# Row maxima turned on their own, and probabilities cast two heads at a time, in the first cross attention of a decoder

## The reference

```python
q = rope(x @ Wq, pos); k = rope((ctx @ Wkv)[..., :512], pos); v = (ctx @ Wkv)[..., 512:]
s = einsum("bqhd,bkhd->bhqk", q, k) / sqrt(16)
o = softmax(s, axis=-1) @ v                      # 32 heads
x = layernorm(x + o @ Wout + bout)
```

## Time and profile before

| | us |
|---|---|
| median of 3 runs (lowest, highest) | 3235.99 (3232.26, 3239.41) |
| the profiled execution | 3238.21 |
| its span, first to last instruction | 3236.4 |
| `xattn0`, from the first exponential to the end of its heads | 776 to 1220 |
| `attn1`, the same with its start | 1880 to 2170 |

### The profile page before, as it was taken

The page is one execution under the profiler, slowest core; times in us unless marked ns, Lnnn a source line. Parts: engine busy times, 40 slices in busy tenths (PEclk is TensorE's granted clock), DMA queues, the critical chain, the costliest instruction groups (busy, mean ns, idle before and its releaser), DMA issues. The chain is left out here.

```text
span 3236.4 us, 64362 instructions
## 1 busy us (share of the span) xinstructions
PE 2811.6 (87%) x24738; PEld 1992.0 (62%) x24738; DVE 2087.0 (64%) x4863; ACT 1765.5 (55%) x3780; POOL 1430.2 (44%) x1539
## 2 busy tenths in 40 slices
PE   5999999967888887999999888989999999965786
PEld 3666666644666665777777666657666666642343
DVE  6677777667777766555555457766555555555896
ACT  4555555546888884333332267755444444454785
POOL 3444444435888884444444425552111112213563
PEclk8999999989999997999999989999999999988998
DMA  5000000000000013000000011002001110022000
GB/s 171 27 1 2 1 1 1 1 19 25 2 2 2 2 47 97 24 8 8 1 1 1 1 57 41 15 2 76 27 27 33 34 40 1 1 80 70 14 20 27
DMA packets 47124, 81.75 MB, mean 25 GB/s; under 512 B 5730, under 2 KB 15972, under 8 KB 46692
## 3 DMA queue, kind: packets, MB, share of 16 engines
q1 hardware_dynamic: 46820, 77.64, 7.3%
HBM read 73.44 MB, written 4.19 MB: 24 GB/s over the span
## 5 line engine op out<-in xcount | busy, mean ns | idle before, releaser
L1146 POOL TENSOR_TENSOR c_pT<-c_prob,c_pT 128x512 f16<-128x512 f32 x256 | 293.3, 1159 | 66.4 <-ACT c_pT L1096 65.7
L2029 POOL TENSOR_TENSOR c_prob<-c_prob,c_inv 128x512 f32<-128x512 f32 x128 | 133.1, 1043 | 301.4 <-DVE c_inv L2247 301.4
L789 DVE SCALAR_TENSOR_TENSOR a_pT<-psT,a_kvh_t,a_pT 128x256 f16<-128x256 f32 (+1 forms) x256 | 94.6, 411 | 168.9 <-ACT a_pT L695 168.9
L1339 ACT ACTIVATE c_prob<-psT 128x512 f32<-128x512 f32 x256 | 156.2, 610 | 73.1 <-PE psT L1268 52.1
L1146 POOL TENSOR_TENSOR a_pT<-a_prob,a_pT 128x384 f16<-128x384 f32 x128 | 120.8, 949 | 156.8 <-ACT a_pT L1096 156.1
L1423 DVE TENSOR_REDUCE c_peak<-psS 128x2 f32<-128x512 f32 x256 | 167.1, 683 | 11.5 <-PE psS L1249 9.3
L1096 ACT CAST c_pT<-c_prob 128x512 f16<-128x512 f32 x256 | 159.9, 625 | 0.0
L2163 ACT ACTIVATE c_prob<-c_prob,c_negmax 128x256 f32<-128x256 f32 x256 | 127.8, 501 | 55.9 <-DVE c_negmax L2239 54.9
L488 POOL TENSOR_TENSOR a_q_rot<-a_q_cos,a_q_sin 128x512 f32<-128x512 f32 x64 | 86.7, 1355 | 160.7 <-DVE a_q_sin L808 160.7
L507 POOL TENSOR_TENSOR a_prob<-a_prob,a_inv 128x128 f32<-128x128 f32 x128 | 52.4, 409 | 221.8 <-DVE a_inv L782 221.8
L1679 POOL TENSOR_TENSOR f_ch<-f_h,f_c 128x256 f32<-128x256 f32 x88 | 76.2, 866 | 141.9 <-DVE f_h L1896 141.7
(11 more groups left out here) (625 smaller groups left out, 11319.9 us busy)
## 6 DMA issues: line engine op xcount, KB each, us to landing
c_feed<-in_L_ffn_w1T SPq DMA_DIRECT2D x16, 512.0 KB, 3.7
c_feed<-in_L_ffn_w2T SPq DMA_DIRECT2D x16, 512.0 KB, 3.7
x_all<-in_x SPq DMA_DIRECT2D x8, 512.0 KB, 7.1
a_ring<-in_L_attn_WqT SPq DMA_DIRECT2D x8, 512.0 KB, 5.3
a_ring<-in_L_attn_WoutT SPq DMA_DIRECT2D x8, 512.0 KB, 3.8
a_feed<-in_L_xattn_Wq SPq DMA_DIRECT2D x8, 512.0 KB, 3.6
c_feed<-in_L_xattn_Wo SPq DMA_DIRECT2D x8, 512.0 KB, 4.2
c_feed<-in_L_ffn_w3T SPq DMA_DIRECT2D x8, 512.0 KB, 3.6
```

Source lines behind the costliest of these rows:

```text
L789: last = dve.scalar_tensor_tensor(pT[1][:, r, m, m * P:N], T[:, m * N + m * P:(m + 1) * N], kvh_t[:, b % 2, m, H + h:H + h + 1], pT[0][:, ...
L1146: pool.tensor_tensor(pT[1][:, c % NPH, :], prob[:, c % NPX, :], pT[0][:, c % NPH, :], ALU.subtract)\
L1339: act.activation(prob[:, c % NPX, :], ST[c % 2][:, 0:EW], ACT.Exp).then_inc(s.e_done, 1)
L2029: pool.tensor_tensor(prob[:, h % NPB, :, :], prob[:, h % NPB, :, :], inv[:, h % NPB, :].rearrange("p (n a) -> p n a", a=1).broadcast_to([P ...
```

## The change

In the layers that are not causal (`by_row`, so `xattn0` alone) the maxima no longer go through `q_stack`. DVE writes them into a tile `peak` of 128 columns per half, eight of which are a group's heads and the rest zero. PE turns this tile (two f32 turns of 128 x 128 for a group), DVE copies the 256 columns to `peak_rows` times -1/1024, and the scores with keys on the partitions get a second product: `pick`, a 128 x 128 tile that is 1024 in the row of the head and zero elsewhere, with `peak_rows`. The copy over `qS` on ACT, the product of `fill_slots` and the clearing of the slot on POOL go. `q_stack` has one buffer instead of two.

ACT casts the probabilities of two heads with one instruction, at even slots (`TOGETHER = 2`), and `prob` has four buffers instead of three. `pv` runs six slots after its head's scores instead of seven.

In `attn1`, `fill_slots` takes the later maximum with one reduction into `late` and writes the slots with two products instead of one.

```diff
-    NPX, NPH = 3, 6
+    NPX, NPH = 3 if causal else 4, 6
+    by_row = not causal
+    NQS = 1 if by_row else 2
+    TOGETHER = 2 if by_row else 1
...
-        q_stack = sc.sb("q_stack", [P, 2, NT, H, 4, D], F16)
+        q_stack = sc.sb("q_stack", [P, NQS, NT, H, 4, D], F16)
-        peak = sc.sb("peak", [P, H, PIECES], F32)
+        peak = sc.sb("peak", [P, 2, NT, P] if by_row else [P, H, PIECES], F32)
+        peak_rows = sc.sb("peak_rows", [P, 2, N], F16) if by_row else None
+        pick = sc.sb("pick", [P, GH, P], F16) if by_row else None
...
         def round_p(eng, copy, c):
-            eng.wait_ge(s.e_done, c + 1)
-            if c >= NPH:
-                eng.wait_ge(s.pv_done, c - NPH + 1)
-            copy(pT[0][:, c % NPH, :], prob[:, c % NPX, :]).then_inc(p_high(c)[0], 1)
+            last = c + TOGETHER - 1
+            eng.wait_ge(s.e_done, last + 1)
+            if last >= NPH:
+                eng.wait_ge(s.pv_done, last - NPH + 1)
+            copy(pT[0][:, c % NPH:c % NPH + TOGETHER, :], prob[:, c % NPX:c % NPX + TOGETHER, :]).then_inc(s.p_hi_act, 1)
...
-                    if kind == "q":
-                        pool.memset(q_stack[:, b % 2, n, :, 3, 0:1], 0.0).then_inc(s.slot_clear, 1)
...
+                def turn_peak_rows(b, g):
+                    pe.wait_ge(s.m_done, b * H + (g + 1) * GH)
+                    for n in range(NT):
+                        last = pe.transpose(bank_of("peak", b, g)[:, n * P:(n + 1) * P], peak[:, g % 2, n, :],
+                                            G.ident[:, :])
+                    last.then_inc(s.bank_ready, 1)
...
-                                         start=True, stop=not causal, skip_group_check=True)
-                        if causal:
+                                         start=True, stop=False, skip_group_check=True)
+                        if by_row:
+                            last = pe.matmul(out, pick[:, h % GH, :], peak_rows[:, h // GH % 2, q0:N], start=False, stop=True,
+                                             skip_group_check=True)
+                        else:
...
                 def q_stack_is_free(b):
-                    if b >= 2:
-                        act.wait_ge(s.bank_ready, use["peak", b - 2, NG - 1] + 1)
+                    if b >= NQS:
+                        act.wait_ge(s.bank_ready, (last_sk(b - 1, "q") if by_row else use["peak", b - 2, NG - 1]) + 1)
...
-                    if 0 <= t - 1 < B * H:
-                        round_p(act, act.copy, t - 1)
+                    if 0 <= t - TOGETHER < B * H and t % TOGETHER == 0:
+                        round_p(act, act.copy, t - TOGETHER)
...
                 def fill_slots(b, g):
                     heads = slice(g * GH, (g + 1) * GH)
                     dve.wait_ge(s.m_done, b * H + (g + 1) * GH)
-                    if causal:
-                        step(dve.tensor_tensor(peak[:, heads, 1], peak[:, heads, 1], peak[:, heads, 2], ALU.max))
-                    dve.tensor_tensor(q_stack[:, b % 2, :, heads, 3, 0], peak[:, heads, 0:NT].rearrange("p h n -> p n h"),
-                                      shift[:, 0:1].rearrange("p (n h) -> p n h", n=1).broadcast_to([P, NT, GH]),
-                                      ALU.mult).then_inc(s.slot_done, 1)
+                    step(dve.tensor_reduce(late[:, :], peak[:, heads, 1:3], X_AXIS, ALU.max))
+                    slots = q_stack[:, b % NQS, :, heads, 3, 0]
+                    scale = shift[:, 0:1].broadcast_to([P, GH])
+                    dve.tensor_tensor(slots[:, 0, :], peak[:, heads, 0], scale, ALU.mult)
+                    dve.tensor_tensor(slots[:, 1, :], late[:, :], scale, ALU.mult).then_inc(s.slot_done, 1)
+
+                def move_peaks(b, g):
+                    dve.wait_ge(s.bank_ready, use["peak", b, g] + 1)
+                    if NG * b + g >= 2:
+                        dve.wait_ge(s.st_ready, (NG * b + g - 1) * GH)
+                    dve.tensor_scalar(peak_rows[:, g % 2, :], bank_of("peak", b, g)[:, 0:N], -1.0 / SHIFT, None, ALU.mult)\
+                        .then_inc(s.bank_dve, 1)
...
-                     "peak": 28, "PV": 7}, G.c0, G.c0.end)
+                     "peak": 28, "PV": 6}, G.c0, G.c0.end)
```

More of the change, by code:

```diff
@@ L994, in small_attention @@
         prob = sc.sb("prob", [P, NPX, EW], F32)
-        peak = sc.sb("peak", [P, H, PIECES], F32)
-        shift = sc.sb("shift", [P, 1], F32)
+        peak = sc.sb("peak", [P, 2, NT, P] if by_row else [P, H, PIECES], F32)
+        late = sc.sb("late", [P, GH], F32) if causal else None
+        shift = None if by_row else sc.sb("shift", [P, 1], F32)
+        peak_rows = sc.sb("peak_rows", [P, 2, N], F16) if by_row else None
+        pick = sc.sb("pick", [P, GH, P], F16) if by_row else None
         inv = sc.sb("inv", [P, NT, GH], F32)
@@ L1060, in frees_bank @@
                 return "act" if sk_uses[n][0] == "q" else "dve"
-            return "act" if kind == "peak" else "dve"
+            return "act" if kind == "peak" and not by_row else "dve"
         use, freed, hi_at, v_at = {}, [], {}, {}
@@ L1120, in _ @@
             def _(pool):
-                pool.memset(shift[:, :], -1.0 / SHIFT).then_inc(s.zeroed, 1)
                 pool.memset(q_stack[:, :, :, :, 3, :], 0.0).then_inc(s.zeroed, 1)
-                pool.memset(k_stack[:, :, :, 3, 1:D], 0.0).then_inc(s.zeroed, 1)
-                pool.memset(k_stack[:, :, :, 3, 0:1], SHIFT).then_inc(s.zeroed, 1)
+                if by_row:
+                    pool.memset(k_stack[:, :, :, 3, :], 0.0).then_inc(s.zeroed, 1)
+                    pool.memset(peak[:, :, :, :], 0.0).then_inc(s.zeroed, 1)
+                else:
+                    pool.memset(shift[:, :], -1.0 / SHIFT).then_inc(s.zeroed, 1)
+                    pool.memset(k_stack[:, :, :, 3, 1:D], 0.0).then_inc(s.zeroed, 1)
+                    pool.memset(k_stack[:, :, :, 3, 0:1], SHIFT).then_inc(s.zeroed, 1)
                 pool.memset(v_ones[0][:, :, :, :, D:VW], 1.0).then_inc(s.zeroed, 1)
@@ L1136, in stack_lo @@
                     pool.wait_ge(s.rot_hi, u + 1)
-                    out, hi = (q_stack[:, b % 2, n, :, 1, :], q_stack[:, b % 2, n, :, 0, :]) if kind == "q" else \
+                    out, hi = (q_stack[:, b % NQS, n, :, 1, :], q_stack[:, b % NQS, n, :, 0, :]) if kind == "q" else \
                         (k_stack[:, n, :, 2, :], k_stack[:, n, :, 0, :])
-                    if kind == "q":
-                        pool.memset(q_stack[:, b % 2, n, :, 3, 0:1], 0.0).then_inc(s.slot_clear, 1)
                     pool.tensor_tensor(out, part[:, u % 2, 0, :].rearrange("p (h d) -> p h d", d=D), hi, ALU.subtract)\
@@ L1311, in _ @@
                         elif kind == "peak":
-                            turn_peaks(b, n)
+                            (turn_peak_rows if by_row else turn_peaks)(b, n)
                         elif kind == "o":
@@ L1350, in stack_hi @@
                     heads = H if kind == "q" else KVH
-                    out = q_stack[:, b % 2, n, :, 0:3:2, :] if kind == "q" else k_stack[:, n, :, 0:2, :]
+                    out = q_stack[:, b % NQS, n, :, 0:3:2, :] if kind == "q" else k_stack[:, n, :, 0:2, :]
                     view = src.rearrange("p (h d) -> p h d", d=D)
@@ L1366, in _ @@
                         turned_stack = kind == "sk" and frees_bank(kind, n) == "act"
-                        if kind in ("x", "o", "v", "kv", "peak") or turned_stack or (kind == "q" and not from_ctx):
+                        turned_peaks = kind == "peak" and not by_row
+                        if kind in ("x", "o", "v", "kv") or turned_stack or turned_peaks or (kind == "q" and not from_ctx):
                             bank = bank_of(kind, b, n)
@@ L1391, in _ @@
                             move_stack(act.copy, b, n).then_inc(s.bank_act, 1)
-                        elif kind == "peak":
+                        elif turned_peaks:
                             act.copy(qS[:, b % 2, GB * n:GB * (n + 1), :],
@@ L1422, in rowmax @@
                     S = SB[a % 2][:, 0:EW].rearrange("p (r m) -> p r m", r=PIECES)
-                    dve.tensor_reduce(peak[:, h, :], S, X_AXIS, ALU.max).then_inc(s.m_done, 1)
+                    group = a // GH
+                    if by_row and group >= 2 and h % GH == 0:
+                        dve.wait_ge(s.bank_ready, use[("peak", *divmod(group - 2, NG))] + 1)
+                    top = peak[:, group % 2, :, h % GH] if by_row else peak[:, h, :]
+                    dve.tensor_reduce(top, S, X_AXIS, ALU.max).then_inc(s.m_done, 1)
                 def fill_slots(b, g):
@@ L1467, in low @@
                     elif kind == "q":
-                        st = q_stack[:, b % 2, n, :, :, :]
+                        st = q_stack[:, b % NQS, n, :, :, :]
                         dve.memset(st[:, :, 3, 0:1], 0.0)
@@ L1531, in _ @@
                             move_stack(dve.tensor_copy, b, n).then_inc(s.bank_dve, 1)
+                        elif kind == "peak" and by_row:
```

(3 more changed lines are left out.)

15 lines of the change are left out of this document (9 added, 6 removed).

## The result

The changed kernel takes 3253.99 us in the median of 5 runs (3246.51 to 3258.48), the kernel before 3235.99 (3232.26 to 3240.19). The ratio is 1.0054, 95% interval [1.0043, 1.0065]: slower by 18 us. The forecast was 3263, its range 3222 to 3286.

What follows compares the result with a forecast made beforehand. No engine was taken as full: the bound moves within each period, through waits among POOL, ACT, PE and DVE. 3.6 us a period summed to +27 on 3236.0, so 3263 us in the median, range 3222 to 3286.

Steps and rivals of the forecast that it cites:

- the ring: First cross attention: low part, exponential, pair cast, low part again takes 2.87 us per pair against 2.44, POOL idling 0.60.
- First cut: Part of each sequence's period from head 0's exponential to head 10's: POOL's idle gaps add +1.3 us, ends 0 and +2.
- Fourth cut: Slots 27 to next head 0: late cast behind Q's projection leaves POOL without work, +1.5 us, between 0 and 2.6.
- Product and peaks: Second cut (head 10 to slot 21): extra matmuls less earlier bank, +0.5 us; third (slots 21 to 27): DVE's copy, +0.3.
- Sum: 3.6 us per period, 25 for seven sequences, +1.3 for the last, 1 for attn1: +27 us in all.
- the DVE stall: Removed DVE product, 229 to 4573 ns, contends with GpSimd; its replacement never stalls, giving back at most about 4 us.
- attn1: The other layer: one tiny DVE instruction more per group, 32 in all, 0 to 7 us of work, taken as 1.
- Start: The 1024-column DVE write and changed memsets before the first stack is turned: between -1 and +1 us, taken as 0.
- Rival (a): ACT is what bounds and its relief wins, half of 38 us counting: 3217 us, chance 0.24.
- Rival (b): Ring as described, but lumps of PE cover it and copies given back pay for PE's steps: about 3236 us, chance 0.12.
- Rival (c): PE becomes the bound outright, 55 us more less at most 14 of turns: 3277 us, chance 0.06.
- Rival (d): The DVE product's stall mattered more than its waits show, 17 us given back in full: 3246 us, no own chance.

Runs made afterwards that it cites:

- e2: Kernel before the change plus the pair cast, four prob buffers and the product with V six slots behind, maxima the old way: 3256.2 us, ratio 1.0067.
- e3: Changed kernel with both heads cast as soon as the second exponential is issued, one slot sooner: 3229.7 us, ratio 0.9984 to the kernel before.
- e6: Changed kernel with six prob buffers instead of four, pair cast left in its place: 3237.1 us, ratio 1.0009 to the kernel before.
- e7: Changed kernel with one cast per head, keeping its four prob buffers: 3221.1 us, ratio 0.9959 to the kernel before.
- e4: Changed kernel without the matmul that adds the maxima to the turned scores, so maxima are not subtracted: 3250.9 us, ratio 1.0051 to the kernel before.
- e8: Kernel before the change with four prob buffers instead of three and nothing else: 3216.1 us, ratio 0.9940.
- e9: Kernel before the change with four prob buffers in the first cross attention and attn1's new fill: 3212.9 us, ratio 0.9940.
- e5: Changed kernel with attn1's old fill, one product of maxima by scale instead of two small ones: 3260.7 us, ratio 1.0076 to the kernel before.
- e1: Changed kernel with single casts, three prob buffers and the product with V seven slots behind, so the new maxima alone: 3233.4 us, ratio 0.9991 to before.
- e10: e9 with the maxima scaled by a constant in the instruction in both layers, one SBUF operand instead of two: 3213.6 us, ratio 0.9937 to before.
- e11: e9 plus the pair cast at odd slots and the product with V six slots behind: 3226.0 us, ratio 0.9971 to before.

## Why the prediction was right, and where its sizes were off

The direction and the main mechanism, the ring, held; some of the smaller terms came out right for other reasons. By its own steps:

- **The ring.** Forecast 2.87 us per pair with 0.60 idle on POOL and a cast of 1.00 to 1.06; found 2.86, 0.58 and 1.04. That this ring is the cause is shown four ways: put alone into before it costs 22 us (e2), and a sooner place (e3), more buffers (e6) or single casts (e7) each take away 17 to 33 us.
- **First cut** +1.3, found +1.2. The gap behind the high stack was put at 1.4; it is 1.47 at 952.33.
- **Fourth cut** +1.5, found +1.5, by an idle time of POOL of 1.46 at 939.43. Together these two are 2.8 in the forecast and 2.8 in e2 (17.2 and 12.2 against 15.9 and 10.7). The fourth is the same without the product (e4) and with six buffers (e6), so the late cast makes it, as forecast.
- **Product and peaks** +0.5 and +0.3, found +0.5 and +0.25 in after's cuts. The numbers are better than the reasons. In the second cut the product costs 1.3 (21.08 against 19.77 in e4) where 1.1 was forecast, the pair cast adds 0.3 (20.86 in e2), which the forecast left out, and the relief is about 1.1 where 0.6 was forecast. In the third cut the forecast blamed DVE's new copy. But e4, which keeps that copy and lacks the product, takes 10.18, less than before's 10.37, so the product makes the increase, and the +0.3 came out by luck. PE's step is 0.96 (957.74 to 958.70 in after) as forecast. The peaks' copy takes 411 to 426 ns with no outlier.
- **Sum.** 3.6 a period was forecast and 3.45 found in plain periods. The whole came to 18 us and not 27. In the stage the seven periods differ by +1.6, -0.8, +3.5, +3.8, +1.8, +3.4, +3.2 and the last sequence by +2.2, together +18.6 (rounded terms) where 26 was forecast. Of the 8 that are missing, 5.9 are in the next point. About 2 are in the first period, which was taken as a full one: by cuts it differs by -0.05, -0.56, -0.05 and +2.2, so the first cut did not grow at all; why is open. The last sequence grew by 0.9 more than forecast.
- **The term that was mis-sized: what before itself loses.** The forecast took every period of before as plain and counted nothing for what the change could give back. The periods with -0.8 and +1.8 are those in which before is long, 61.75 and 59.20 us where a plain one takes 57.53: 4.2 and 1.7, or 5.9 us. They have two causes. The first is the DVE stall, which the forecast bounded at 4 us and counted as nothing: the first cut of the long period takes 18.47 instead of 15.93, 2.5 more, and that includes a stretch at half the clock right behind the stall (836.38 to 839.79). In before's timeline of DVE and of POOL:

```profile
831.50 4.57 DVE L1430 TENSOR_TENSOR c_q_stack<-c_peak,c_shift 128x16 f16<-128x16 f32 x1
835.94 0.68 DVE L1423 TENSOR_REDUCE c_peak<-psS 128x2 f32<-128x512 f32 x1
```

```profile
829.10 1.26 POOL L1132 TENSOR_TENSOR c_part<-c_part 128x512 f32<-128x512 f32 x1
830.33 2.26 POOL L1146 TENSOR_TENSOR c_pT<-c_prob,c_pT 128x512 f16<-128x512 f32 x2
832.54 0.23 POOL L1140 MEMSET c_q_stack<- 128x32 f16 x1
832.62 1.14 POOL L1141 TENSOR_TENSOR c_q_stack<-c_part,c_q_stack 128x512 f16<-128x512 f32 x1
833.73 2.25 POOL L1146 TENSOR_TENSOR c_pT<-c_prob,c_pT 128x512 f16<-128x512 f32 x2
```

  It ends at 836.07, and POOL's unbroken work at 835.98. The second cause is TensorE's clock, of which the forecast had no term. In both long periods the granted clock is 0.50 for 3.41 us in the fourth cut, where PE does the projection of Q without a pause, and that cut takes 12.36 instead of 10.68 us, 1.7 more each time. The rows are the two stretches and the fourth cut of the first of these periods:

```profile
877.34:880.75 3.41, 3.41 (x10) 1.21 (x9) 1.41 (x2) 1.84 (x3) 3.41 (x4) 0.50 0.00 0
1051.42:1054.83 3.41, 3.41 (x14) 1.22 (x11) 1.59 (x2) 2.02 (x3) 3.41 (x4) 0.50 0.00 0
876.37:888.73 12.36, 12.07 (x128) 7.51 (x128) 6.98 (x15) 8.15 (x14) 10.60 (x11) 0.86 0.01 1
```

  After has four such stretches in its seven periods, all in first cuts, where they cost nothing, and none in a fourth cut. Why they moved is open. That the change removed the stall by replacing the instruction is not shown either. None of the seven kernels with the new maxima has a copy of them above 426 ns or a stall of this kind. But the old product does not always stall: its longest is 4.57 us in before and 5.69 in e8, and 1.22 in e2 and 1.28 in e9.
- **attn1** was put at +1 for the additional small instruction. Its exponentials are 4.0 us shorter in after. Two pairs of kernels differ in the fill alone: from e5 to after the new one saves 3.1 us (271.9 to 268.8), from e8 to e9 1.2 (272.9 to 271.7). But e1 and e6 have the new fill and 271.6 and 271.7, and after, e3, e4 and e7 268.8 to 268.9. The sign of the term was wrong; what decides its size stays open, with one profile of each kernel.
- **Start.** Taken as 0, found +1.2; the bound was +1. It is no scatter: the stretch takes 68.9 to 70.1 us in the seven kernels with the new maxima and 67.1 to 67.8 in the others. DVE's write of 1.45 us at 706.34 stands ahead of DVE's memset of `c_kS` at 708.70; that it is the cause is not shown.
- **Rival (a), ACT bounds.** It fell. Its condition was that POOL's other work takes more than about 0.5 us of idle per pair; in after's plain heads the 0.58 stands uncovered. e7 says it plainly: 15 us more ACT work, 33 us less time.
- **Rival (b), lumps cover.** It fell: all four cuts grew.
- **Rival (c), PE outright.** It fell: e1, with the product in, is no slower than before, and e4, with the product gone, is 3 us from after.
- **Rival (d), the stall is worth up to 17 us.** It fell: the cut that holds the stall is 2.5 us longer than a plain one.

The DVE stall also bears on a rule that the prediction used. The Trainium skill, SBUF - State Buffer, section Who interferes with whom, has a DVE instruction with two SBUF inputs contend with a GpSimd instruction that reads SBUF, and a copy or tensor_scalar contend when it runs in a two-port mode. The forecast's use of it, that a copy from PSUM never stalls, agrees with 411 to 426 ns. The long one in e10 is a tensor_scalar with one SBUF input, so only the second clause could cover it; no trace shows the mode it ran in. By the page the blocked side waits for one instruction of the other; in the rows below it waits for six.

A version that beats both kernels is e8, or e9 and e10, which no run can tell from each other: 3213 to 3216 us, 0.6% under before. A fourth buffer in attn1 as well was not tried.

## What to carry to other kernels

Merging two instructions saves an engine its fixed part per instruction, but an engine in a ring of buffers is not judged by its busy time. Draw the ring (buffer freed, written, cast, consumed, freed), add the intervals, and compare with the consumer's own time for that many buffers; a merged step comes later by a whole element, and here it took more buffers (e6) or an earlier place (e3) to hide that. When a change bundles a buffer with another edit, try the buffer alone: here it gave 18 us and the bundle lost 18. And before summing differences per period, look at every period of the kernel before, and at the granted clock in each: two long ones, by a stall of one instruction and by two short drops of the clock, hid 5.9 of the 8 us by which the forecast of the stage was off.

## What the runs showed of the hardware

- **A small DVE instruction can stand still for as long as POOL works.** In before one took 4.57 us and ended 0.09 after the last of a series on POOL; in e8 one took 5.69. The longest, in e11, took 7.35 and ended 0.09 after POOL's unbroken work of 894.91 to 905.22:

```profile
897.96 7.35 DVE L1438 TENSOR_TENSOR c_q_stack<-c_peak,c_shift 128x16 f16<-128x16 f32 x1
```

  In e10 it is a product by a constant, with one SBUF operand (timelines of DVE, then of POOL):

```profile
823.04 0.69 DVE L1424 TENSOR_REDUCE c_peak<-psS 128x2 f32<-128x512 f32 x1
823.77 5.67 DVE L1435 TENSOR_SCALAR c_q_stack<-c_peak 128x16 f16<-128x16 f32 x1
```

```profile
822.61 2.27 POOL L1147 TENSOR_TENSOR c_pT<-c_prob,c_pT 128x512 f16<-128x512 f32 x2
824.83 0.23 POOL L1141 MEMSET c_q_stack<- 128x32 f16 x1
824.90 1.15 POOL L1142 TENSOR_TENSOR c_q_stack<-c_part,c_q_stack 128x512 f16<-128x512 f32 x1
826.02 3.36 POOL L1147 TENSOR_TENSOR c_pT<-c_prob,c_pT 128x512 f16<-128x512 f32 x3
832.73 1.15 POOL L1147 TENSOR_TENSOR c_pT<-c_prob,c_pT 128x512 f16<-128x512 f32 x1 [3.35 <-ACT c_pT L1097]
```

  It ends at 829.44, POOL's row at 829.38. It outlasted six POOL instructions in a row, none longer than 1.2 us, while the maximum from PSUM just before it, also beside POOL, took its usual 0.69. The median of the same instruction is 374 ns, so most of them get through; what decides which one starves is open.
- **Less work for PE came with a lower granted clock.** In the last sequence's 47 us it is 0.92 in after, 0.79 in e4, which differs by the missing product alone, and 0.78 in before (the rows are after's and e4's):

```profile
1183.00:1230.00 47.00, 39.59 (x591) 29.96 (x588) 21.33 (x43) 33.01 (x49) 39.02 (x36) 0.92 0.01 2
```

```profile
1184.00:1231.00 47.00, 36.10 (x539) 25.44 (x538) 22.81 (x43) 33.56 (x51) 40.04 (x36) 0.79 0.01 2
```

  Over the exponentials of the last sequence it is 0.89 to 1.00 in the six kernels with the product, and 0.75 to 0.89 in the others. So part of what e4 saves in PE's work goes back into slower matmuls, here and in the second cuts shown at e4.
- **A short drop of the clock costs what PE is needed for.** A stretch of 3.41 us at 0.50 costs 1.7 us in the fourth cut (12.36 against 10.68 in before; 12.35 against 10.67 in e9), where PE is busy throughout, 1.5 in e4's second cut, and nothing in after's first cut (17.12 with it, 17.11 without), where the ring sets the pace. PE was busy 8.45 to 8.46 of the 10.37 us ahead of the fourth cut in before, whether the clock then fell or not, so these rows do not tell why it fell.
